# Attention programs without a loop on three engines, and the sums of the four-tile chunk one visit later

## What is computed

```python
xn = _layernorm(x, axis=-1)                      # x: (2, 2048, 1024) f32
q = (xn @ wq).reshape(b, s, 32, 32)              # k, v: 8 heads, each used by 4 query heads
scores = jnp.einsum('bihd,bjhd->bhij', q, k) * SCALE
scores = jnp.where(causal, scores, jnp.finfo(scores.dtype).min)
attn = jax.nn.softmax(scores, axis=-1)
out = jnp.einsum('bhij,bjhd->bihd', attn, v).reshape(b, s, 1024) @ wo
g = _silu(_L0_ffn_ref(xn, ...))
return x + out * g
```

## Time and profile before

| | |
|---|---|
| median of 3 runs | 3469.17 us (3466.11 to 3469.25) |
| the profiled execution's own time | 3466.9 us |
| its span, first to last instruction | 3465.1 us |
| mean granted TensorE clock | 0.974 |
| busy: PE, PE's weight loads, DVE, ACT, POOL | 96%, 64%, 54%, 42%, 39% |
| attention, first to last `cols_ps` | 680 to 2685 us |

### The profile page before, as it was taken

How to read it: one execution, slowest core, us unless ns; L and a number is a source line. 1 busy time by engine, 2 the same in 40 slices (tenths; PEclk the granted TensorE clock), 3 DMA queues, 4 the chain that set the end, 5 groups by cost and what they waited for, 6 DMA issues and landing times. The chain is left out here.

```text
span 3465.1 us, 54971 instructions
## 1 busy us (share of the span) xinstructions
PE 3311.4 (96%) x18048; PEld 2203.3 (64%) x18048; DVE 1887.9 (54%) x4622; ACT 1448.7 (42%) x2658; POOL 1357.7 (39%) x549
## 2 busy tenths in 40 slices
PE   6999999799999999999999999999999799989999
PEld 5888888555555555555545555555553688878887
DVE  6333332487767767767766767767772322223333
ACT  3121211156656656656655656656665211110000
POOL 0000000056766766676676676667667000000000
PEclk9999999899999999999999999999999899999999
DMA  6555554445656656556555565656655444445554
GB/s 225 164 159 165 178 166 134 116 102 119 142 112 137 131 126 132 121 127 137 125 123 129 129 134 121 137 118 133 137 136 131 157 154 140 142 134 180 192 192 174
DMA packets 283519, 494.67 MB, mean 143 GB/s; under 512 B 40864, under 2 KB 156576, under 8 KB 263328
## 3 DMA queue, kind: packets, MB, share of 16 engines
q1 hardware_dynamic: 260256, 333.04, 32.5%
q0 software_dynamic: 20736, 151.00, 21.8%
q10 hardware_dynamic: 2304, 7.87, 0.6%
HBM read 205.03 MB, written 134.74 MB: 98 GB/s over the span
## 5 line engine op out<-in xcount | busy, mean ns | idle before, releaser
L902 POOL TENSOR_TENSOR added<-added,probs 128x2048 f32<-128x2048 f32 (+3 forms) x320 | 1184.1, 3700 | 848.7 <-PE o_ps L973 814.8
L1081 DVE TENSOR_REDUCE row_max<-rows_ps 128x1 f32<-128x512 f32 x1536 | 994.3, 683 | 269.7 <-PE rows_ps L935 267.8
L1055 ACT ACTIVATE probs<-cols_ps 128x512 f32<-128x512 f32 x1728 | 927.3, 611 | 354.9 <-PE cols_ps L1017 317.7
L1085 DVE CUSTOM_DVE_ANT_0 masked_rows<-rows_ps,tri 128x128 bf16<-128x128 f32 (+3 forms) x1024 | 485.4, 483 | 236.1 <-PE rows_ps L935 203.5
L935 PE MATMUL rows_ps<-k_st,q_st 96*128 96x512 f32 (+3 forms) x1536 | 538.1, 379 | 44.0 <-DVE row_max L1085 17.4
L1017 PE MATMUL cols_ps<-q_st,k_st 97*128 97x512 f32 x1248 | 522.5, 425 | 0.6
L973 PE MATMUL o_ps<-probs,v_st 128*32 128x512 f32 (+3 forms) x4224 | 433.0, 527 | 0.0
L1017 PE MATMUL cols_ps<-q_st_last,k_st 97*128 97x512 f32 x928 | 390.1, 434 | 3.8 <-ACT dma_added L1055 2.1
L935 PEld LDWEIGHTS rows_ps<-k_st,q_st 96*128 96x128 f32 x1536 | 302.2, 197 | 143.8 <-DVE row_max L1081 47.6
L935 PE MATMUL rows_ps<-k_st,q_st_last 96*128 96x512 f32 (+3 forms) x1024 | 374.6, 390 | 7.7 <-DVE row_max L1085 4.1
L1017 PEld LDWEIGHTS cols_ps<-q_st,k_st 97*128 97x128 f32 x1248 | 238.5, 191 | 171.5 <-issue 109.5
(11 more groups left out here) (113 smaller groups left out, 3820.0 us busy)
## 6 DMA issues: line engine op xcount, KB each, us to landing
dma_added<-probs POOLq DMA_DIRECT2D x144, 1024.0 KB, 7.5
q_st<-scratch_q_hi SPq DMA_DIRECT2D x96, 256.0 KB, 5.6
x_sb<-in_x SPq DMA_DIRECT2D x32, 512.0 KB, 4.1
scratch_xt_hi<-xt_hi SPq DMA_DIRECT2D x32, 512.0 KB, 6.0
scratch_xt_lo<-xt_lo SPq DMA_DIRECT2D x32, 512.0 KB, 6.7
scratch_q_hi<-out_hi SPq DMA_DIRECT2D x64, 256.0 KB, 2.5
scratch_q_lo<-out_lo SPq DMA_DIRECT2D x64, 256.0 KB, 2.9
l_sb<-scratch_l_inv SPq DMA_DIRECT2D x256, 64.0 KB, 5.5
```

The source lines that it names most:

```text
L902: nc.gpsimd.tensor_tensor(total[:, :, q0:CH], total[:, :, q0:CH], probs_of(c, j)[:, :, q0:CH], ALU.add).then_inc(pool_added, 1)
L1055: nc.scalar.activation(probs_of(c, j)[:, :, i * P:(i + 1) * P], cols_ps[cols_slot(AT_T[t])][:, :].rearrange("p (h q) -> p h q", h=NREP), A ...
L1081: nc.vector.tensor_reduce(into, bank[:, :], AX.X, ALU.max).then_inc(rows_free, 1)
L1085: nc.vector.tensor_tensor_reduce(masked_rows[rows_slot(k)][:, 0:keys], bank[:, 0:keys], tri[:, CH - keys:CH], 1.0, MASKED, ALU.add, ALU.ma ...
```

## The change

It does two things.

- `over_stages` with its loop is gone; `over_stages_once` takes its name and is used by all engines. DVE, SP and POOL have all 16 groups written out. No jump, no register arithmetic for the semaphore values and addresses; waits of `wait_apart` stay instructions of their own. The instructions in the program grow from 1676 rows to 3530 on DVE, from 269 to 500 on POOL, from 572 to 995 on SP.
- The sums of chunk 4 move from event number 20 to 28, from behind the first visit of chunk 8 to behind its second. With them the whole chain moves by eight numbers: the gather from 24 to 32, the reciprocal from 32 to 40, the put from 33 to 41, the spread from 37 to 45, the scaling from 43 to 51, the store from 45 to 53. The other chunks stay.

```diff
 for _c in range(CPB):
-    _t = weighed_at((_c + 1) % CPB, 0) + (0 if _c + 1 < CPB else NTG)
+    _t = weighed_at((_c + 1) % CPB, 0 if _c else 2) + (0 if _c + 1 < CPB else NTG)
     event(_t, "Y", _c)
...
-        def over_stages(engine, run):
-
-            for c in range(PEEL):
-                run(Step(0, 0), c, [op for op in FIRST_STAGES[c] if not of_group_before(op)])
-            with engine.Fori(0, NPAIR - 1) as pair:
-                for c in range(PEEL, CPB):
-                    run(Step(pair, 0), c, STAGES[c])
-                for c in range(CPB):
-                    run(Step(pair, 1), c, STAGES[c])
-                for c in range(PEEL):
-                    run(Step(pair + 1, 0), c, STAGES[c])
...
-        def over_stages_once(run):
+        def over_stages(run):
             for g in range(NG):
                 for c in range(CPB):
...
-            over_stages(sp, run)
+            over_stages(run)
...
-            over_stages(pool, run)
+            over_stages(run)
...
-            over_stages(dve, run)
+            over_stages(run)
```

More of the change, by code:

```diff
@@ L724, in attend @@
         PEEL = 3
-        def over_stages(engine, run):
-            for c in range(PEEL):
-                run(Step(0, 0), c, [op for op in FIRST_STAGES[c] if not of_group_before(op)])
-            with engine.Fori(0, NPAIR - 1) as pair:
-                for c in range(PEEL, CPB):
-                    run(Step(pair, 0), c, STAGES[c])
-                for c in range(CPB):
-                    run(Step(pair, 1), c, STAGES[c])
-                for c in range(PEEL):
-                    run(Step(pair + 1, 0), c, STAGES[c])
-            last = NPAIR - 1
-            for c in range(PEEL, CPB):
-                run(Step(last, 0), c, STAGES[c])
-            for c in range(CPB):
-                run(Step(last, 1), c, [op for op in STAGES[c] if not of_group_after(op)])
-            for c in range(PEEL):
-                run(Step(NPAIR, 0), c, [op for op in STAGES[c] if of_group_before(op)])
-        def over_stages_once(run):
+        def over_stages(run):
             for g in range(NG):
@@ L1025, in run @@
                         row_sums(n, *op[1:])
-            over_stages_once(run)
+            over_stages(run)
         @block.scalar
```

## The result

| | before | after |
|---|---|---|
| median | 3469.21 us (3466.11 to 3469.97, 4 runs) | 3405.65 us (3402.33 to 3409.13, 4 runs) |
| ratio | | 0.9819, 95% interval 0.9802 to 0.9836 |
| the profiled execution's own time, its span | 3466.9, 3465.1 us | 3404.86, 3403.1 us |
| mean granted TensorE clock | 0.974 | 0.985 |

The kernel is 63.6 us faster; 55 were forecast, and the time lies inside the stated range of 3386 to 3446 us. All lines of the attention stand 20 lower in the kernel after (the sums at L970, the adding DMA at L892).

The account below looks back on a forecast made before the run. PE, busy 96% of the span, bounds the kernel; only its idle time or slowed clock can be won. 118.5 + 1.0 + 0.6 = 120.1 us for 14 groups, 1681.4 instead of 1736.2, gives 3414 us; range 3386 to 3446.

Parts of the forecast that it names:

- Part 1, the loop: In the attention's groups: six jumps go, the six groups become like the eight others, no better; 29.6 us gained.
- The sums of chunk 12: In each group, PE's wait there for POOL's adds becomes 0.1 to 1.4 us, taken as 1.0; group 11 had 1.83.
- the 0.6 us for slow adding DMAs: Added to each group because 24 of 144 adding DMAs take 8.4 us or more and delay POOL.
- rival D: Straight code is fetched late: one stall like the jump's in every pair of groups, 3443 us; chance 0.04.
- rival A: PE's wait for the sums of chunk 12 goes entirely: 118.5 us a group, 3389 us; chance 0.20.
- rival B: Moving the sums of chunk 4 gives nothing, only jumps are gained: 3440 us; chance 0.20, shared with a few caught groups.
- The DVE side: DVE's 1.38 us wait for the gather of chunk 8 shrinks; worth -0.3 to +0.3 us a group, taken as nothing.
- The spread of chunk 4: It lands with chunk 12's first adding DMA; after the scaling the second goes out 0.9 to 1.6 us sooner.
- The put of chunk 8: It goes out some 0.8 us behind the second adding DMA, is caught and lands with it, 7.7 us from issue.
- Rival C: Spread of chunk 8 lands only with the third adding DMA: about 129 us a group, 3539 us; six groups or more, 0.06.

Follow-up runs that it names:

- groups 7 and 10: Two groups of the run on the kernel after with the store of chunk 4 again ahead of the gather of chunk 8: 3477.51 us, ratio 1.002.
- the last experiment: The kernel before, with its loop, with the gather of chunk 8 moved ahead of the store of chunk 4: 3459.3 us, ratio 0.9962.

## Why the prediction was right, and where it was not

*Part 1, the loop: right, in size and in place.* 29.6 us were forecast; without the second part it is 29. The former jump groups became like the others, no better (121.7 and 122.5 us). Straight code cost nothing that shows: rival D is out.

*The sums of chunk 12: right.* The forecast was 1.0 us in the usual group and 0.6 for slow adding DMAs, 1.6 together; it is 1.70 in the mean. The usual groups (2, 3, 6, 7, 10, 11, 13, 14) wait 0.93 us, the six others 1.8 to 4.5. In 5 and 9 the first adding DMA took 9.3 and 9.2 us, as I had it. In 4, 8 and 12 it is something else, below, and in 1 it is both (9.65 us). So that the 0.6 us for slow adding DMAs came out near is in part luck: 5 and 9 alone give 2.7 us over the 14 groups of the 8.4 that I had put there. The wait did not go (rival A), and the second part gave more than nothing (rival B).

*The DVE side: the term that was mis-sized.* I took it as nothing, within 0.3 us a group. It is 0.8: group 11 without its wait took 118.5 us before and takes 118.49 - 0.75 = 117.7 now, and group 14 the same. I had also the wrong hand on it. The gather of chunk 8 was not late before for the 0.37 us in which the store is issued. The store waits for the scaling of chunk 4, and so does the first adding DMA on POOL, which then went out first; so the gather came 0.86 us behind that DMA (2118.45) and landed with it:

```profile
2118.75 0.37 SPq L885 DMA_DIRECT2D scratch_o<-o_sb  x1
2119.31 0.61 SPq L872 DMA_DIRECT2D l_few<-l_sb  x1
```

DVE waited 1.2 to 3.1 us for it in every group, and PE paid in waits too short for a bracket. After the change the gather is caught still (0.57 us behind the first adding DMA), but that DMA is over 1.6 us before the reciprocal asks. The runs in pairs show what this is worth: alone without a jump nothing, because POOL is the later one and takes it back (the gather ahead of the store, without the loop); in the six groups with the jump 2.6 us each in the mean (the same, with the loop), enough for all of the 2.1 us that the moved sums gained there. That it is the same microseconds in both runs is likely and not shown, since the single groups differ by several. Only together with an earlier POOL does it count in all groups. A term that is nothing alone was not nothing in the sum.

The account for the 14 groups against the 1681.4 us forecast: 0.8 x 14 = 11.2 us less by the DVE side; 1.4 more at the sums of chunk 12; 2.3 more for a wait that I did not foresee, PE for the row of the last chunk's queries (1.42 us in group 3, 0.86 in group 10), whose write now goes out right behind the late spread of chunk 8 on SP (2085.42 behind 2084.95 in group 11; before, 2133.09 behind 2130.66); and 1.7 lost to the clock in group 1. That is 1675.6, and 1676.0 is measured.

```profile
1136.96 0.50 PE L997 MATMUL cols_ps<-q_st_last,k_st 97*128 97x512 f32 x1 [1.42 <-DMA q_st_last<-row]
```

*The spread of chunk 4: a wrong step with little harm.* I had it land with the adding DMA, near 54 us into the group. Its four DMAs went out at 45.3 to 46.6 us in group 11, the adding DMA at 46.5, and all four were through by 48.5, the last one though it went out 0.03 us behind the adding DMA. POOL's scaling did not wait at all. That it did not make the usual wait shorter than forecast is because the second adding DMA has to wait for the end of the first anyhow (0.28 us in group 11). In groups 1, 4, 8 and 12 the last spread went out 1.4 to 4.6 us behind the adding DMA and was caught; there the step is right, and these are four of the six groups with long waits. Group 1, the worst:

```profile
869.45 0.88 POOL L892 DMA_DIRECT2D dma_added<-probs  x1 [3.85 <-ACT probs L1035]
...
880.06 1.28 POOL L904 TENSOR_TENSOR o_sb<-o_sb,l_sb 128x512 f32<-128x512 f32 x1 [4.56 <-DMA l_sb<-scratch_l_inv]
```

*The put of chunk 8: right.* It went out 1.34 us behind the second adding DMA (0.8 forecast), and the spread that waits for it 5.9 us later, with that DMA's end. The last of the four spreads is then issued 1.6 us ahead of the third adding DMA in group 11 (1.4 forecast).

*Rival C: right as a mechanism, dearer in the forecast than on the chip.* Moved behind the third adding DMA, the spread costs a group 127.2 us, where I had 129; and with seven of the 14 groups caught, and the first and the last, the kernel is 19 us slower than before; I had said that it decides from six. In the kernel after it happened in no group.

The Trainium skill (DMA: Bandwidth & Descriptors, Queues, rings and completion order) has two rules here. By the one that I weighed, each DMA engine takes turns between its queues; by that a gather would not care whether it goes out 0.01 or 0.10 us behind an adding DMA, and the rows of groups 7 and 10 speak against it as a rule for when a transfer is done. The other, in the paragraph on ordering, says that a transfer's semaphore write lands only after all earlier writes of that DMA engine, across its queues. That one agrees with what is seen: the transfer is reported when the big one ends. I had not weighed it; it would have backed rival C's price, not changed the sum. Whether the data itself was there earlier no run here shows.

## What to carry to other kernels

Look at which transfers are issued behind a large one, on any queue, and who waits for them; a tenth of a microsecond in the issue order can decide between 2 and 7 us (groups 7 and 10 above). Where an engine waits for a side engine that is always late by the same amount, ask for the result later in the program before making the side engine faster: here that gave 34 us for one number in a table and one more semaphore. And cost two edits together where each removes one of two waits that cover each other; one alone showed nothing in the one setting and 2 us a group in the other.

## What the runs showed of the hardware

- At a jump back in its program DVE sat idle without a releaser for 4.8 to 7.1 us (five of the six jumps in the kernel before: 4.98, 6.87, 6.91, 4.78, 6.97; up to 7.07 with SP and POOL written out); on SP and POOL jumps cost nothing that the time shows (3470.37 with them written out against 3470.21 on the same chip).
- A small gather issued 0.09 us or more behind a 1 MB adding DMA was reported only with that one's end; at up to 0.02 us behind, it came through. The edge is not the same for all transfers. Over all 14 profiles every put up to 0.42 us behind landed within 1.4 to 2.6 us, and every put from 0.59 us on landed only with the end; none lies between. For the spreads it is no sharp edge. The last of the four landed within 1.9 to 2.6 us when it went out up to 0.4 us behind, within 2.0 to 8.0 us from 0.4 to 1.0 us behind, and from 1.0 us on with the end or in the half microsecond before it.
- In the kernel after and the six other runs with moved sums of chunk 4 and the same lists of adds, the first adding DMA of chunk 12 took 9.1 to 9.8 us in groups 1, 5 and 9, and 6.9 to 8.0 in the others, each time. In the run with one add less on POOL it took 7.5 to 8.2 us in these three, and in the kernel before the slow ones (over 8 us) were in groups 5, 9 and 13. Why these are slow is open; no run touched their addresses.
- PE idling for 4.52 us was followed by a window of 5 us at a granted clock of 0.66 in the kernel after, where waits of up to 2.72 us left it at 1.00. The length of one wait does not decide it: behind waits of 2.03 us (group 6 with DVE alone written out) and 2.21 us (group 3 with only the loop gone) such windows have 0.66 and 0.67, and behind one of 3.27 us (group 7 of the last experiment) 1.00. What decides it these runs do not show.
